# Self attention with one product for queries and keys and interleaved softmax, and a norm stage shared by two engines

## The reference, cut to what matters

```python
x = x + L1_xattn(layernorm(x), ctx, ctx, Wq, bq, Wk, bk, Wv, bv)   # cross attention
x = x + L1_attn(layernorm(x), Wq, Wk, Wv)                          # self attention
x = x + L1_ffn(layernorm(x), w_gate, w_up, w_down)                 # quantized, comes last

def L1_attn(X, Wq, Wk, Wv):          # Wq, Wk: 512 x 64, Wv: 512 x 512
    Q, K, V = X @ Wq, X @ Wk, X @ Wv
    scores = where(causal, Q @ K.T, -inf)            # per sequence of 64 rows
    return softmax(scores / sqrt(64)) @ V
```

## Time and profile before

| | |
|---|---|
| Median of three runs | 1812.0 us (1810.86 to 1813.96) |
| The profiled execution | 1809.76 us, its span 1808.0 us |
| Query stage (`cross1_queries`), in the span | 1263.2 to 1323.7 us |
| Self attention (`self1`), in the span | 1471.1 to 1544.2 us |
| TensorE clock granted, mean | 0.955 of full speed |

### The profile page before, as it was taken

How to read it: one execution, slowest core, us unless ns; L and a number is a source line. 1 busy time by engine, 2 the same in 40 slices (tenths; PEclk the granted TensorE clock), 3 DMA queues, 4 the chain that set the end, 5 groups by cost and what they waited for, 6 DMA issues and landing times. The chain is left out here.

```text
span 1808.0 us, 34242 instructions
## 1 busy us (share of the span) xinstructions
PE 1614.5 (89%) x14024; PEld 829.6 (46%) x14024; DVE 1179.7 (65%) x1991; ACT 915.4 (51%) x1261; POOL 800.1 (44%) x406
## 2 busy tenths in 40 slices
PE   5999999999999999986699899898989989699349
PEld 2445555555555555543435543354434444344124
DVE  6588888888888888863555477697312222627881
ACT  1387787877877877764362133311012122228750
POOL 2277887888788888863028234422000000003310
PEclk9999999999999999989799799999999999799779
DMA  3589999999999999996327522243839941000001
GB/s 133 142 151 190 196 190 194 194 191 190 194 192 191 195 188 189 193 167 145 90 76 234 214 74 71 87 132 109 330 125 399 388 180 65 1 1 1 0 1 47
DMA packets 517543, 273.31 MB, mean 151 GB/s; under 512 B 443776, under 2 KB 495488, under 8 KB 514320
## 3 DMA queue, kind: packets, MB, share of 16 engines
q1 hardware_dynamic: 517392, 271.18, 62.5%
HBM read 138.74 MB, written 22.54 MB: 89 GB/s over the span
## 5 line engine op out<-in xcount | busy, mean ns | idle before, releaser
L493 POOL TENSOR_TENSOR x<-x_prob,x 128x1604 bf16<-128x1604 f32 x120 | 388.1, 3234 | 145.5 <-ACT x L648 145.5
L771 DVE TENSOR_REDUCE x_negmax<-x_score 128x1 f32<-128x1604 f32 x128 | 233.6, 1825 | 15.2 <-PE x_score L534 5.1
L630 ACT ACTIVATE x_prob<-x_score,x_negmax 128x1604 f32<-128x1604 f32 x128 | 204.8, 1600 | 44.2 <-DVE x_negmax L771 39.3
L517 PE MATMUL x_ring<-x_ctx_hi,wk_split 128*128 128x400 bf16 (+1 forms) x1024 | 216.2, 333 | 0.3 <-DVE x_kT L707 0.3
L517 PE MATMUL x_ring<-wv_split,x_ctx_hi 128*128 128x512 bf16 (+1 forms) x832 | 214.2, 380 | 0.0
L707 DVE SCALAR_TENSOR_TENSOR x_kT<-x_ring,bk,x_kT 128x400 bf16<-128x400 f32 (+1 forms) x256 | 162.1, 634 | 32.0 <-ACT x_kT L619 24.0
L648 ACT CAST x<-x_prob 128x1604 bf16<-128x1604 f32 x120 | 183.0, 1525 | 0.0
L713 DVE TENSOR_TENSOR x_v<-x_ring,x_v 128x512 bf16<-128x512 f32 (+1 forms) x208 | 143.7, 691 | 52.9 <-ACT x_v L623 50.1
L619 ACT ACTIVATE x_kT<-x_ring,bk 128x400 bf16<-128x400 f32 (+1 forms) x196 | 116.2, 593 | 71.6 <-PE x_ring L517 70.8
L550 PE MATMUL x_pv<-x_pT,x_v 128*64 128x128 bf16 (+1 forms) x3328 | 119.0, 222 | 29.2 <-DVE x_kT L734 17.7
L623 ACT CAST x_v<-x_ring 128x512 bf16<-128x512 f32 (+1 forms) x148 | 86.7, 586 | 97.9 <-PE x_ring L517 97.7
(11 more groups left out here) (330 smaller groups left out, 2595.9 us busy)
## 6 DMA issues: line engine op xcount, KB each, us to landing
y_ctx<-in_ctx SPq DMA_DIRECT2D x16, 1664.0 KB, 10.5
y_ctxT<-in_ctxT SPq DMA_DIRECT2D x16, 1601.0 KB, 14.0
x_stage<-in_ctxT SPq DMA_DIRECT2D x48, 400.0 KB, 4.4
x_q_rows<-q_rows SPq DMA_DIRECT2D x64, 128.0 KB, 3.1
m_xT<-in_L_ffn_w SPq DMA_DIRECT2D x16, 512.0 KB, 4.6
ffn_w_parts<-m_xT SPq DMA_DIRECT2D x32, 256.0 KB, 2.7
x_stage<-in_ctxT SPq DMA_DIRECT2D x16, 401.0 KB, 4.9
f_w<-ffn_w_parts SPq DMA_DIRECT2D x4, 1024.0 KB, 10.6
```

Source lines behind the costliest of these rows:

```text
L493: pool.tensor_tensor(ph[:, g % 2, 1, 0:NKP], prob[:, g % 2, :], ph[:, g % 2, 0, 0:NKP], ALU.subtract).then_inc(pl_done, 1)
L517: last = pe.matmul(out_, lhs, rhs, start=(i == 0), stop=(i == len(steps) - 1))
L630: nc.scalar.activation(prob[:, g % 2, :].rearrange("p (c n) -> p c n", n=QW), scores, ACT.Exp, bias=nmax[:, g % 2:g % 2 + 1], accum_out=rs ...
L771: dve.tensor_reduce(nmax[:, pair % 2:pair % 2 + 1], scores, mybir.AxisListType.XY, ALU.max, negate=True).then_inc(max_done, 1)
```

## The change

In words:

1. A new class `SharedNorm` takes the place of `Norm` in the two stages. DVE writes xhat tiles 0 to 3, ACT tiles 4 to 7 (`Identity` with a scale and a shift that one small DVE instruction makes). The banks are emptied by ACT for tiles 2, 4, 6 and by DVE for tiles 0, 1, 3, 5, 7. There are six banks in place of two.
2. In the query stage the products wait for the first four tiles, for six at the third group and for eight at the fifth. The two halves of the `bk` row are computed alternately, into partition 0 of one bank and partition 32 of another.
3. In self attention, `Wq` and `Wk` lie side by side, so that one group of four products 128 rows high makes queries and keys of one half.
4. PE's order of self attention is new (below). The mask, maximum and exponentials work by halves of four tiles, and ACT does the exponentials after value tiles 0 and 1. Outputs use two banks in turn in place of four.

```diff
+class SharedNorm(Norm):
+    HALF = NT // 2
+    BY_SCALAR = (2, 4, 6)
+    BY_VECTOR = (0, 1, 3, 5, 7)
...
+    def turn_on_tensor(self, pe, t):
+        if t < self.HALF:
+            pe.wait_ge(self.s_hat, t + 1)
+        else:
+            pe.wait_ge(self.s_hat_act, t - self.HALF + 1)
+        if t >= len(self.banks):
+            self.wait_turned(pe, t - len(self.banks) + 1)
...
+    def on_scalar(self, nc, act):
+        self.root_on_scalar(nc, act)
+        act.wait_ge(self.s_shift, 1)
+        for t in range(self.HALF, NT):
+            nc.scalar.activation(self.xhat[:, t, :], self.x[:, t, :], ACT.Identity, bias=self.shift[:, t:t + 1],
+                                 scale=self.rstd[:, t, :]).then_inc(self.s_hat_act, 1)
+        for t in self.BY_SCALAR:
+            act.wait_ge(self.s_turned, t + 1)
+            nc.scalar.copy(self.xT[:, :, t * P:(t + 1) * P],
...
+    def on_vector(self, dve):
+        self.small_on_vector(dve)
+        dve.scalar_tensor_tensor(self.shift[:], self.meanvar[:, :, 0], -1.0, self.rstd[:, :, 0], ALU.mult,
+                                 ALU.mult).then_inc(self.s_shift, 1)
+        self.hat_on_vector(dve, range(self.HALF))
+        for t in self.BY_VECTOR:
+            dve.wait_ge(self.s_turned, t + 1)
+            dve.tensor_copy(self.xT[:, :, t * P:(t + 1) * P],
...
@@ cross1_queries
-        norm = Norm(k, ctx, "yq", x, ident, banks[0:2], xT)
+        norm = SharedNorm(k, ctx, "yq", x, ident, banks[0:2] + banks[4:8], xT)
...
-            pe.wait_ge(norm.s_xT, NT)
             for n, (m, c) in enumerate(groups):
+                if n in (0, KD):
+                    norm.wait_turned(pe, NT // 2 * (c + 1))
+                if n == 2:
+                    norm.wait_turned(pe, 6)
...
-            for c in range(2):
-                for j in range(KD):
-                    last = pe.matmul(banks[4 + c][0:1, :], bk[:, j:j + 1], qT[:, j, 512 * c:512 * c + 512],
+            for j in range(KD):
+                for c in range(2):
+                    last = pe.matmul(banks[4 + c][32 * c:32 * c + 1, :], bk[:, j:j + 1], qT[:, j, 512 * c:512 * c + 512],
...
@@ self1
-        wq = k.sb(ctx, "s_wq", [P, 2, KD, DQ])
+        wq = k.sb(ctx, "s_wq", [P, KD, 2, DQ])
...
-        norm = Norm(k, ctx, "sn", x, ident, banks[0:2], xT)
+        norm = SharedNorm(k, ctx, "sn", x, ident, banks[0:6], xT)
...
+            def queries_keys(c):
+                norm.wait_turned(pe, HALF * (c + 1))
                 for j in range(KD):
-                    last = pe.matmul(banks[2 + n][0:DQ, :], wq[:, n // 2, j, :],
-                                     xT[:, j, 512 * (n % 2):512 * (n % 2) + 512], start=(j == 0), stop=(j == KD - 1))
+                    last = pe.matmul(banks[6 + c][:], wq[:, j].rearrange("p a n -> p (a n)"),
+                                     xT[:, j, 512 * c:512 * c + 512], start=(j == 0), stop=(j == KD - 1))
...
+            def scores(c):
+                pe.wait_ge(s_qc, 2 * c + 2)
...
+            def turned_probabilities(c):
+                for t in range(HALF * c, HALF * c + HALF):
+                    pe.wait_ge(s_e, t + 1)
...
+            def outputs(t):
+                pe.wait_ge(s_vc, t + 1)
+                pe.wait_ge(s_tc, t // HALF + 1)
+                if t >= 2:
+                    pe.wait_ge(s_x, t - 1)
+                pe.matmul(banks[2 + t % 2][:], pT[:, t, :], v[:, t, :], start=True, stop=True).then_inc(s_o, 1)
...
@@ self1, vector engine
-            for n in range(4):
-                dve.wait_ge(s_q, n + 1)
-                dve.tensor_copy(qkT[:, n // 2, 512 * (n % 2):512 * (n % 2) + 512], banks[2 + n][0:DQ, :]).then_inc(s_qc, 1)
+            for c in range(2):
+                dve.wait_ge(s_q, c + 1)
+                for n in range(2):
+                    dve.tensor_copy(qkT[:, n, 512 * c:512 * c + 512], banks[6 + c][DQ * n:DQ * n + DQ, :]).then_inc(s_qc, 1)
...
+                dve.tensor_tensor(sc[:, part, :], banks[4 + c][:].rearrange("p (t n) -> p t n", t=HALF),
+                                  low[:].unsqueeze(1).broadcast_to([P, HALF, P]), ALU.add).then_inc(s_sc, 1)
```

More of the change, by code:

```diff
@@ L118, in on_vector, with small_on_vector @@
     def on_vector(self, dve):
+        self.small_on_vector(dve)
+        self.hat_on_vector(dve, range(NT))
+    def small_on_vector(self, dve):
         before = NT if self.loaded else 0
@@ L141, in on_vector, with hat_on_vector @@
         dve.wait_ge(self.s_var, 6)
-        for t in range(NT):
+    def hat_on_vector(self, dve, tiles):
+        for t in tiles:
             dve.tensor_scalar(self.xhat[:, t, :], self.x[:, t, :], self.meanvar[:, t, 0:1],
@@ L148, in on_tensor, with turn_on_tensor @@
             self.turn_on_tensor(pe, t)
-    def turn_on_tensor(self, pe, t):
-        pe.wait_ge(self.s_hat, t + 1)
+    def turn_on_tensor(self, pe, t, ready=None):
+        pe.wait_ge(*(ready or (self.s_hat, t + 1)))
         if t >= len(self.banks):
@@ L1830, in values @@
                 last.then_inc(s_v, 1)
[L1832 to L1853, removed]
+            def scores(c):
+                pe.wait_ge(s_qc, 2 * c + 2)
+                for t in range(HALF * c, HALF * c + HALF):
+                    tile = slice(t * P, (t + 1) * P)
+                    last = pe.matmul(banks[4 + c][:, P * (t % HALF):P * (t % HALF) + P], qkT[:, 0, tile], qkT[:, 1, tile],
+                                     start=True, stop=True)
+                last.then_inc(s_s, 1)
@@ new lines, in _ @@
+            for t in range(HALF + 2):
+                norm.turn_on_tensor(pe, t)
+            pe.wait_ge(s_in, 48)
+            queries_keys(0)
+            for t in range(HALF + 2, NT):
+                norm.turn_on_tensor(pe, t)
+            queries_keys(1)
+            scores(0)
+            values(0)
+            scores(1)
+            values(1)
+            values(2)
+            values(3)
+            turned_probabilities(0)
+            values(4)
+            turned_probabilities(1)
+            outputs(0)
@@ L1855, in _, with value @@
+            outputs(1)
+            values(5)
+            outputs(2)
+            outputs(3)
+            values(6)
+            outputs(4)
+            outputs(5)
+            values(7)
+            outputs(6)
+            outputs(7)
         @block.scalar
         def _(act):
-            norm.on_scalar(nc, act)
-            for t in range(NT):
+            def value(t):
                 act.wait_ge(s_v, t + 1)
                 nc.scalar.copy(v[:, t, :], banks[t % 2][:]).then_inc(s_vc, 1)
-            act.wait_ge(s_b, 1)
@@ L1866, in _ @@
+            norm.on_scalar(nc, act)
+            value(0)
+            exps(0)
+            value(1)
+            exps(1)
+            for t in range(2, NT):
+                value(t)
         @block.vector
```

65 lines of the change are left out of this document (41 added, 24 removed).

## The result

| | before | after |
|---|---|---|
| Median | 1811.4 us (4 runs, 1810.7 to 1814.0) | 1788.05 us (4 runs, 1786.7 to 1791.9) |
| Profiled execution, its span | 1809.76, 1808.0 us | 1786.74, 1785.0 us |
| Ratio after / before, 95% interval | | 0.9876 (0.9862 to 0.989) |

The change made the kernel 1.24% faster. Forecast were 1792.6 us and a gain of 19.4. A second group of runs, under Experiments, gave 1811.0 against 1789.2 us, ratio 0.989 (0.9864 to 0.9916). One of its eleven runs of the kernel before, 1875.4 us at a mean clock of 0.897, belongs to a slower state and is left out of the ratio.

The account below looks back on a forecast made before the run. PE was taken to bound both edited stages, with DVE ending self attention. Gains of 15.0 there, 1.0 for the query stage's norm and 3.4 for `bk` sum to 19.4, giving 1792.6 us; own range 1789.5 to 1795.5.

Parts of the forecast that it names:

- A: Query stage: the `bk` halves do not run side by side; gain 16.0, time 1796.0 us; chance 0.10.
- B: Self attention: DVE becomes the bound through copies and two output banks; 4 us lost, 1796.6 us; chance 0.11.
- C: Self attention: clock falls in PE's new pause and stays low; slower, up to 1834 us; chance 0.03.
- D: Both stages: the norm gives nothing back, inputs or copies being late; 3.1 us less, 1795.7 us; chance 0.08.
- both ranges: Whole kernel: the forecast's own range, 1789.5 to 1795.5 us, and the 8 in 10 range, 1788.5 to 1797.5 us.
- The start of the first product: Self attention: the shared norm lets the first queries-and-keys product start at 1479.3 instead of 1481.44.
- PE from the second queries-and-keys product: Self attention: 3.46 for that product, 37.9 for PE's remaining work and 0.9 for changes; PE ends at 1527.1.
- The term of 0.1 for each of nine changes between kinds: Self attention: each change between kinds of PE product costs 0.1, 0.9 us in all, ends 0 and 1.8.
- the tail: End of self attention: after output 6 at 1526.2, 0.1, then DVE tiles of 1.39 and 1.45, ending at 1529.2.
- `bk`: 3.4 forecast: Query stage: the two halves of the `bk` row run side by side, halving 6.9 us; gain 3.4.
- The norm: 1.0 forecast: Query stage: PE pauses of 1.36 in all go, the shift costs 0.20; gain 1.0, between 0 and 1.6.
- The floor at `yq_bv`: Query stage: input `yq_bv` lands at 1271.76 and L1530 waits for it, which limits the norm's gain.

Follow-up runs that it names:

- bk_half_by_half: Changed kernel with the `bk` row written half by half, eight records per position, positions kept; query stage 57.8 us.
- filled: Changed kernel with value tiles 0 and 1 around the second queries-and-keys product, scores together, both turned-probability halves behind value tile 4; self attention 56.2 us.
- exps_late: Changed kernel with its order of self attention undone, exponentials after all eight value copies, two output banks kept; self attention 66.0 us.
- filled_spread: Changed kernel with value tile 0 before the second queries-and-keys product, scores together, turned probabilities behind value tiles 3 and 4; self attention 55.7, median 1788.1 us.
- after_again: The changed kernel run once more, in the second group; median 1789.2 us, ratio to before 0.989, self attention 57.3 us.
- six_banks: Kernel before with six norm banks in both stages and the query stage's staged waits, no second engine; query stage 59.2, self attention 72.1 us.
- plain_norm: Changed kernel with DVE making all xhat tiles and ACT emptying all six banks; median 1789.1 us, ratio to before 0.9882.

## Why the prediction was right, and where its sizes were off

**The chain.** Right in every link. PE sets the pace from the first product to the last output, the exponentials and their table load are covered, the clock stays up, inputs are in time, DVE frees the output banks in time. Rivals A, B, C and D fall: `bk` in 3.6 us, the one PE pause at 0.87 (forecast 0.8), clock 1.00, and the norm's gain kept. What was off are sizes, and with them the number left both ranges by a little. The range was also added up too narrowly: the bounds that it names give 1789.3 to 1796.1.

**Self attention, 15.0 forecast, 16.6 found.** Two terms make most of it.
- The start of the first product. I had 8.14 us behind the stage's start (1479.3 less 1471.16), the trace has 7.53. The other five profiles with the same norm have 7.58 (bk_half_by_half), 7.90 (filled), 8.07, 8.10 and 8.13 (exps_late, filled_spread, after_again). So most of this 0.6 is luck of one execution: tiles 0 to 5 took 4.29 there at a mean clock of 0.64, and 5.07 in after_again at 0.52:

```profile
1467.80:1472.70 4.90, 4.85 (x24) 4.86 (x25) 3.34 (x6) 3.37 (x6) 0.00 (x0) 0.52 1.08 417
```

- PE from the second queries-and-keys product. I had 3.46 + 37.9 + 0.9 = 42.3, and it took 41.5 (1478.04 to 1519.57). The term of 0.1 for each of nine changes between kinds, 0.9 in all, was mis-sized. Where all 128 rows and columns of the array stay in use, a change costs nothing: value tile 4 to the turned probabilities, 1498.28 to 1501.72, is 8.0 records of 0.43. The scores, with 64 rows of the array, are another case. From 1478.04 to 1497.85 are 19.81 us, and at an even pace they would be 18.95 (40 records of 0.429, and 16 of 0.111, which is what eight more scores cost between 1.09 and 1.98). Of the 0.86 left, 0.08 stand in the first record behind the pause, and each of the two visits to the scores costs 0.39, half on the way in and half on the way out. The Trainium skill, TensorEngine Tiling, Key Properties, says that a change of tiling mode drains the array; the trace agrees in so far as these changes cost time and the others none. So the added visit cost the 0.4 that I had charged for it, and the 0.5 for the other changes was nothing. The remaining 0.2 come mainly from 20.87, a busy time whose last record already overlaps the next by 0.16.

The rest is tiles 6 and 7 with the pause behind them, 0.1 shorter than forecast together, and the tail, 0.15 shorter.

The price of rival D was wrong. Its 3.1 us count the 2.1 by which the first product starts earlier, but the sum itself gives 2.0 of them back behind that product, for tiles 6 and 7 and the pause. So the forecast's norm was worth 0.1 in self attention, not 2.1. Measured in this way, the second product's start less 3.43 for the first, the changed norm stands at 9.5 to 10.1 after the stage's start (four profiles), against 10.3 before and 9.45 in six_banks, which waits for all eight tiles. The early start pays only where the pause is filled, as in filled_spread.

**Query stage, 4.4 forecast, 5.1 found.** `bk`: 3.4 forecast, 3.42 measured. The norm: 1.0 forecast, 1.7 found (L1593 starts 8.43 after the stage's start instead of 10.16). I had counted the pauses that the timeline names, 1.36, less 0.20 for the shift, which is 1.16, and then wrote 1.0. The shift cost 0.1, and PE's eight tiles went from start to start in 5.21 us, 0.45 less than the busy times of before (3.42 + 1.12 + 1.12). A turned record lasts 0.27 at the full clock but the next starts 0.11 after it, so each of the three pauses cost 0.16 more than its idle time; small waits between records add to this, and a clock that rose later in the changed kernel takes some back. The floor at `yq_bv` held as a mechanism but not as a number: that transfer lands at other times in other executions, and four of the later profiles show PE waiting for it, by 0.18 to 0.69.

**The stretches that nobody edited.** 1.0 us of the 23.0 by which the two spans differ comes from the batches between. In the fourteen profiles, none of which edits this stage, it lasted 146.2 to 149.9 us, so the 147.2 before and the 146.2 after are draws from a scatter of several us. The two extremes in rows, after first:

```profile
1318.88:1465.09 146.21, 129.38 (x824) 66.05 (x824) 32.72 (x56) 32.32 (x58) 0.00 (x0) 0.99 0.72 284
```

```profile
1321.51:1471.45 149.94, 132.54 (x824) 66.68 (x824) 32.65 (x57) 32.35 (x58) 0.00 (x0) 0.97 0.70 277
```

The second is plain_norm. With the same count of products it has 3.2 us more of busy PE at a lower mean clock. On DVE's timeline a steady tile of this stage takes 17.4 us in both; two intervals differ, the first (12.6 against 11.1) and one in the middle (19.4 against 17.4), and there plain_norm's clock was 0.79 and 0.89, where after had 0.88 and 1.00:

```profile
1381.51:1396.51 15.00, 13.29 (x72) 5.99 (x70) 4.08 (x7) 1.69 (x4) 0.00 (x0) 0.89 0.98 386
```

So these two differ by the clock. It fell in the middle behind two PE pauses of 1.01 and 0.46 us: the four records of `y_wout` there took 3.64 instead of 1.98. But the kernel before has a pause of 1.01 at the same place and keeps 1.98, so why it fell, the runs don't say.

One part is no scatter. PE waits eight times in this stage for DVE's `y_o`. In the seven kernels with the shared norm the wait is 0.66 each time; in the seven with the plain norm it is 1.01 at the third batch and 0.77 at two others, 5.8 us in place of 5.3 in all. The waits of plain_norm and of after_again (us in total, times, longest):

```profile
PE y_turn L1764 <- DVE y_o L1822: 5.8, 8, 1.0
```

```profile
PE y_turn L1759 <- DVE y_o L1817: 5.3, 8, 0.7
```

At the third, DVE starts `y_o` 0.40 us after its wait for the semaphore is over in the kernels with the plain norm, and 0.05 after it in the others, and stands idle in between. plain_norm and after_again differ in the norm alone, so this 0.6 us goes with the `SharedNorm` program, although it is another stage; why, the runs don't show, and the medians don't resolve it. The forecast put nothing there.

Over the profiles with the same stage (self attention 56.7, 56.8 and 57.3 against 73.4, query stage 55.5 against 60.8) the change is worth some 21.7 us, near the 21.8 of the second group's medians; the 23.4 of the first is more than the change. The forecast's 19.4 was short by 2.3, and its median by more because of this scatter, for which I had allowed 1 us, and because the profiled run lay 1.3 and not 2.2 under the median.

**What each edit is worth,** undone or done alone: one queries-and-keys product 6.8 us of PE; the order of self attention 8.8 from the first product on; the `bk` row 3.4; six banks with staged waits 1.5 in the query stage; six banks 0.8 in self attention (where the product starts 9.45 and not 10.3 after the stage's start), of which the changed kernel, with its wait for four tiles and the pause that follows, has 0.2 to 0.8; the second engine in the norm nothing that these runs can tell in the edited stages. In those two stages the parts add up to 20.7 to 21.3, against the 21.7 of the whole, which is within the scatter. The shared norm's program has 0.6 more in the stage between.

## What to carry to other kernels

Where PE is the bound of a stage, look for products that fill only part of its output rows, and put two of them on different positions, by turns; it is worth as much as joining them. Work that waits on another engine at the end of a stage (a softmax) belongs between independent products: it hides the wait, and it saves the clock that a pause costs after it. Before a second engine is given part of a job, give the first more buffers and let the consumer start at half, with work at hand for the pause that this can open.

## What the runs showed of the hardware

- 32-bit products at different positions overlap also when they are not strictly by turns, but not over runs of eight records as over runs of four: 3.54 us by turns, 5.24 in two runs of eight, 6.96 on one position.
- A change between products that use 128 rows and columns of the array and products that use fewer costs 0.2 us each way at the full clock (0.39 a visit of the scores; from the keys, 64 columns, to the values, the first two steps are 0.52 and 0.53 where 0.43 is the pace). Changes of kind at the full size cost nothing.
- The same DVE instruction (`y_o` of the third batch) started 0.40 us after its wait was over in seven kernels with one norm program and 0.05 after it in seven with the other, in a stage that neither edits. The cause is open.
- How soon the clock rises differs between executions of the same instructions. The outputs after the pause, 16 records, took 9.46, 9.49, 9.47, 8.56, 8.50 and 8.16 us in six kernels with that stretch as before.
- ACT needs 0.73 us for an xhat tile of 128 x 512 from SBUF (2.94 for four), DVE 0.47 (3.74 for eight); from PSUM ACT's copy is the quicker, 0.58 against DVE's 0.69.
